# Four GNN layers in one kernel: the graph products of the second layer's next iteration are issued inside the LSTM rounds, and the third layer begins inside the last of them

## The reference, cut to what matters

```
h = relu(layernorm(x));  x = x + L0(h, adj)        # layer 1: graph product, two linear maps with batch norm
h = relu(layernorm(x));  x = x + L1(h, adj)        # layer 2: below
h = relu(layernorm(x));  x = x + L2(h, adj)        # layer 3: U = eigenvectors of the Laplacian of adj
h = relu(layernorm(x));  x = x + L3(h, adj, adj)   # layer 4: three graph products with widths 256, 512, 128

def L1(x, adj):
    h = relu(adj @ (x @ Wg0 + bg0))
    h = relu(adj @ (h @ Wg1 + bg1))
    for p in 1, 2, 3, 4:                            # windows of p neighbouring nodes
        last = LSTM_p(windows of h, p steps)        # gates i, f, g, o from Wih, Whh
        h[:, last node of each window] = last
    return h

def L2(x, adj):  U = eigh(L_norm)[1];  return U @ (relu((U.T @ x) @ W1 + b1) @ W2 + b2)
```

## Time and profile before

| | |
|---|---|
| median of 3 runs | 1040.38 us (1039.38 to 1042.43) |
| the profiled execution: its own time | 1039.46 us |
| its span, first to last instruction | 1037.7 us |
| busy: PE / PEld / DVE / ACT / POOL | 862.0 / 573.9 / 585.2 / 528.8 / 333.5 us |
| chain that ended last | PE 57%, DVE 26%, POOL 7%, ACT 6%, issue 3% |

### The profile page before, as it was taken

How to read it: one execution, slowest core, us unless ns; L and a number is a source line. 1 busy time by engine, 2 the same in 40 slices (tenths; PEclk the granted TensorE clock), 3 DMA queues, 4 the chain that set the end, 5 groups by cost and what they waited for, 6 DMA issues and landing times.

```text
span 1037.7 us, 12401 instructions
## 1 busy us (share of the span) xinstructions
PE 862.0 (83%) x3721; PEld 573.9 (55%) x3721; DVE 585.2 (56%) x3105; ACT 528.8 (51%) x962; POOL 333.5 (32%) x404
## 2 busy tenths in 40 slices
PE   2678487498879899798857858896899999999998
PEld 1444233353558546684435723575756857857856
DVE  5899867876865877488997886202503303303101
ACT  1466365375464755657526445455545545545531
POOL 1333101016555266525736316674301201201000
PEclk9999889598899999999978889998899999999999
DMA  7000000000000000000000000000000100100101
GB/s 322 0 2 1 0 0 1 1 1 1 1 1 1 1 0 2 1 1 1 0 0 1 1 1 1 1 0 1 1 1 1 41 1 1 42 0 1 42 1 40
DMA packets 2963, 13.32 MB, mean 13 GB/s; under 512 B 465, under 2 KB 465, under 8 KB 2641
## 3 DMA queue, kind: packets, MB, share of 16 engines
q1 hardware_dynamic: 2896, 12.54, 3.0%
HBM read 8.35 MB, written 4.19 MB: 12 GB/s over the span
## 4 chain that ended last, share of the span: by engine, by line
PE 57%; DVE 26%; POOL 7%; ACT 6%; issue 3%; DMA 0%; SPq 0%; DVEq 0%; ACTq 0%; POOLq 0%
PE PS L401 56%; POOL BIG L881 6%; DVE ST L1530 2%; ACT T L784 2%; DVE stats L1502 1%; ACT BIG L823 1%; DVE Fq L1322 1%; DVE seg L1323 1%; ACT T L773 1%; ACT BIG L815 1%; DVE T L1626 1%; DVE mv L1509 1%; POOL sc L861 1%; DVE sc L1063 1%; DVE vcol L1060 1%
## 5 line engine op out<-in xcount | busy, mean ns | idle before, releaser
L401 PE MATMUL PS<-BIG,wts 128*128 128x512 f32 (+2 forms) x1264 | 443.2, 507 | 41.7 <-POOL BIG L881 21.3
L401 PEld LDWEIGHTS PS<-BIG,wts 128*128 128x128 f32 x1264 | 244.4, 198 | 207.4 <-issue 123.7
L881 POOL TENSOR_TENSOR BIG<-BIG 128x256 f32<-128x256 f32 (+2 forms) x272 | 255.3, 944 | 273.2 <-ACT BIG L815 208.0
L815 ACT ACTIVATE BIG<-PS,lbias 128x256 f32<-128x256 f32 (+2 forms) x312 | 166.1, 559 | 125.7 <-PE PS L401 124.6
L1641 DVE TENSOR_TENSOR X<-X,PS 128x512 f32<-128x512 f32 x64 | 43.5, 683 | 148.7 <-PE PS L401 87.1
L722 ACT ACTIVATE BIG<-PS 128x1024 f32<-128x1024 f32 x64 | 65.5, 1024 | 88.5 <-PE PS L401 88.5
L722 ACT ACTIVATE T<-PS 128x512 f32<-128x512 f32 x96 | 55.3, 593 | 100.5 <-PE PS L401 100.3
L730 ACT ACTIVATE T<-X,shift,rstd 128x128 f32<-128x128 f32 x192 | 78.3, 481 | 43.7 <-DVE shift L1518 43.7
L401 PE MATMUL PS<-T,wts 128*128 128x512 f32 x192 | 97.3, 637 | 0.7 <-ACT T L722 0.4
L1663 DVE TENSOR_TENSOR T<-PS,wts 128x512 f32<-128x512 f32 x16 | 11.1, 692 | 150.6 <-PE PS L401 150.6
L869 POOL TENSOR_SCALAR rstd<-mv 128x4 f32<-128x4 f32 x48 | 10.9, 228 | 225.3 <-DVE mv L1509 225.3
(11 more groups left out here) (303 smaller groups left out, 1154.3 us busy)
## 6 DMA issues: line engine op xcount, KB each, us to landing
X<-x_in SPq DMA_DIRECT2D x1, 4096.0 KB, 12.6
out<-X SPq DMA_DIRECT2D x16, 256.0 KB, 2.0
wts<-w_in SPq DMA_DIRECT2D x1, 3605.5 KB, 21.7
cst<-cst_in SPq DMA_DIRECT2D x1, 419.0 KB, 3.3
AA<-adj_in SPq DMA_DIRECT2D x2, 16.0 KB, 2.0
```

What stands on the lines that cost most here:

```text
L401: return nc.tensor.matmul(o, l, r, start=start, stop=stop)
L815: nc.scalar.activation(LB[:, q, {"i": I_, "g": G_, "f": F_, "o": O_}[g], 0:n], PS[:, 3 * q + rank[q] % 3, 0:n], ACT.Tanh if g == "g" else ...
L881: nc.gpsimd.tensor_tensor(out, a, b, op).then_inc(pool_set[q], 1)
```

## The change

1. TensorE: the graph stage of iteration i+1 has no place of its own any more. Its 16 products, the four `turn` of i+1 and the four `turn_h` of i-1 are tasks that are issued within the rounds of iteration i, as the table TASKS says: half 0 of (r, q) stands behind the second gate, half 1 behind the last. All tasks write bank 7 (`task_bank`); a task waits until the engine that reads the one before it has done so (`held`). Iteration 0's graph stage stays ahead of round 0.
2. H gets a second buffer (H1, odd iterations).
3. ScalarE: the batch norm (`bn`) of the next iteration stands in round 0, the normed input in round 4, two chunks behind each set's gates, the copies and relus behind gates.
4. VectorE: the adds, biases and the next layer norm are placed for the new order. In iteration 0 the adds and stats stand ahead of the 32nd reflection, not among its instructions, and GpSimd computes the roots.
5. Layer 3's first layer norm: its stats stand in VectorE's twist, its roots on GpSimd ahead of round 7 of iteration 3 (LAST_ROOTS), its normed input on ScalarE in rounds 9 and 10. The product with BDU waits for the last tanh alone; the last four `turn_h` stand behind it, in banks of their own.
6. PACE_GRID from [40, 32] to [50, 38], PACE_TWIST from 27 to 32, PACE_SCAN from 13 to 15; SHORT_ROUND (1.6 on the clock for each set of a short round) is gone.

```
+TASKS = {
+    (0, 1, 1): ("turn", 0), (1, 0, 0): ("turn", 1), (1, 0, 1): ("turn", 2), (1, 1, 0): ("turn", 3),
...
+    (4, 1, 1): ("agg", 0), (5, 0, 0): ("agg", 1), (5, 0, 1): ("agg", 2), (5, 1, 0): ("agg", 3),
...
+NORMED = {(4, 0): (0, 1), (4, 1): (2, 3)}
+LAST_NORMED = {(9, 1): (0, 1), (10, 0): (2, 3)}
+LAST_ROOTS = 7
-PACE_GRID = [40.0, 32.0]
-PACE_TWIST = 27.0
-PACE_SCAN = 13.0
+PACE_GRID = [50.0, 38.0]
+PACE_TWIST = 32.0
+PACE_SCAN = 15.0
-SHORT_ROUND = 1.6
...
+            def task(j, name, k):
+                if held[0]:
+                    before, what, c = held[0]
+                    if what in ("agg", "agg2"):
+                        pe.wait_ge(act_done[c], C_ACT.at(before, DONE_BY[what]))
+                    else:
+                        pe.wait_ge(dve_done[c], C_DVE.at(before, DONE_BY[what]))
+                product(j, name, k, task_bank)
+                held[0] = (j, name, k)
...
+                            if at == 1 and 0 in todo:
+                                task(*todo[0])
+                        if 1 in todo:
+                            task(*todo[1])
...
                     else:
-                        for c in range(NK):
-                            pe.wait_ge(dve_done[c], C_DVE.end)
+                        for q in range(2):
+                            pe.wait_ge(act_set[q], R_ACT.start(ITER))
                     tiles(bank(k), k, T0[:, k, :], BDU[:, :])
+                if i == 0:
+                    pe.wait_ge(dve_done[NK - 1], C_DVE.end)
+                    for k in range(NK):
+                        product(ITER - 1, "turn_h", k, odd_bank(k))
...
             for i in range(ITER):
                 for r, (p, s, part) in enumerate(LSTM):
+                    if i == ITER - 1 and r == LAST_ROOTS:
+                        for k in range(NK):
+                            layer_norm_roots(0, k, D_POOL, D_DVE)
```

More of the change, by code:

```diff
@@ L146, in d_order @@
[L146 to L151, removed]
+GRAPH = ["agg", "g0", "agg2", "g1"]
+C_PE = Order(B_PE.end, [(0, n) for n in ["turn"] + GRAPH]
+             + [(j, n) for i in range(ITER) for j, names in ((i + 1, ["turn"]), (i - 1, ["turn_h"]), (i + 1, GRAPH))
+                if 0 <= j < ITER for n in names])
+C_ACT = Order(B_ACT.end, [(i, n) for i in range(ITER) for n in ["bn", "norm", "aggT", "relu0", "aggT2", "h"]])
@@ new lines, with d_order @@
+C_DVE = Order(B_DVE.end, [(0, n) for n in ["add"] + LN + ["bias0", "bias1"]]
+              + [(j, n) for i in range(ITER) for j, names in ((i + 1, ["add"]), (i - 1, ["add_h"]), (i + 1, ["bias0", "bias1"]))
+                 if 0 <= j < ITER for n in names])
+def d_order(before, front, middle, rest, ahead=(), begun=()):
+    steps = [(0, n) for n in ahead] + [(0, n) for n in begun]
+    for i in range(ITER):
+        steps += [(i, n) for n in front if (i, n) not in steps] + [(i - 1, n) for n in middle if i] + [(i, n) for n in rest]
@@ new lines, with tasks @@
+NORMED = {(4, 0): (0, 1), (4, 1): (2, 3)}
+SCALED = {(0, 0): (0, 1), (0, 1): (2, 3)}
+LAST_NORMED = {(9, 1): (0, 1), (10, 0): (2, 3)}
+LAST_ROOTS = 7
+DONE_BY = {"turn": "add", "turn_h": "add_h", "agg": "aggT", "g0": "bias0", "agg2": "aggT2", "g1": "bias1"}
+def tasks(i, r, q):
+    for part in range(2):
+        if (r, q, part) in TASKS:
+            name, k = TASKS[r, q, part]
+            j = i - 1 if name == "turn_h" else i + 1
+            if 0 <= j < ITER:
+                yield part, j, name, k
@@ L183 @@
 R_PE, R_ACT, R_POOL = lstm_steps()
+LAST_GATES = [f"{g}{len(LSTM) - 1}" for g in gates(1)[1:]]
 LEAD = 1
@@ L581, in lstm @@
                 for r, (p, s, part) in enumerate(LSTM):
+                    there[i, r, "round"] = clock[0]
                     for q in range(2):
-                        x, n = lstm_in(H, q, p, s, part)
+                        x, n = lstm_in(H(i), q, p, s, part)
+                        todo = {half: (j, name, k) for half, j, name, k in tasks(i, r, q)}
                         if r == 0:
@@ L788, in _, with bn @@
-            bn(0)
-            norm(0)
-            for i in range(ITER):
-                for k in range(NK):
-                    copy(k, T1[:, k, 0:CH], l1_bank(k), C_PE.at(i, "agg"))
-                for k in range(NK):
+            def bn(i, k):
+                act.wait_ge(pe_done[k], B_PE.end if i == 0 else C_PE.at(i - 1, "g1"))
+                nc.scalar.activation(T1[:, k, 0:CH], Y2[:, i * SG + k * CH:i * SG + (k + 1) * CH], ACT.Identity,
+                                     bias=bnv[:, 13:14], scale=bnv[:, 12:13]).then_inc(act_done[k], 1)
@@ L805, in _ @@
+            for name in GRAPH:
+                for k in range(NK):
+                    after(0, name, k, l1_bank(k))
+            for i in range(ITER):
                 rank = [0, 0]
+                late = []
                 for r, (p, s, part) in enumerate(LSTM):
-                    if r == NORM_ROUND and i + 1 < ITER:
-                        norm(i + 1)
                     for q in range(2):
-                        _, n = lstm_in(H, q, p, s, part)
+                        _, n = lstm_in(H(i), q, p, s, part)
@@ L1641, in add @@
                 v.tensor_tensor(x, x, src, ALU.add).then_inc(dve_done[k], 1)
+            for k in range(NK):
+                add(0, k, l1_bank(k), C_PE.at(0, "turn"))
+                dve.wait_ge(dve_done[k], C_DVE.at(0, "add"))
+                for _ in stats_of(0, k, C_DVE):
+                    pass
+                if k:
+                    shift_of(0, k - 1, C_POOL)
+            shift_of(0, NK - 1, C_POOL)
             l1[0] = l1_instructions()
@@ L1654, in _ @@
             for k in range(NK):
-                dve.wait_ge(dve_done[k], C_DVE.end)
-                for _ in stats_of(0, k, D_DVE, ""):
-                    pass
-            for k in range(NK):
-                shift_of(0, k, D_POOL, "")
+                add(ITER - 1, k, odd_bank(k), D_PE.at(0, "turn_h"))
             for i in range(ITER):
```

254 lines of the change are left out of this document (142 added, 112 removed), and 3 rows, old and new, of the table TASKS.

## The result

The kernel after takes 991.57 us (median of 4 runs, 991.47 to 992.19), the one before 1039.88 us on the same chip. The ratio is 0.9534, 95% interval 0.9515 to 0.9554: 48 us faster. The forecast was 996.0 us, range 980 to 1018, so it was right in sign, case and range, and 4 us too slow. Experiments ran on several chips; they are compared by their ratios to the kernel before on their own chip and by the spans of their profiled executions (before 1037.7, after 989.8).

A forecast was written before the change was run, and what follows sets the result against it. The prediction took the stage to be bound by TensorE's order, with VectorE close behind at its end. From the profiled 1039.46 us, gains of 56.4 and costs of 12.5 gave 996 us, range 980 to 1018.

The forecast's parts named there:

- Borders: Between iterations, TensorE no longer waits for the last h, the relu into H or VectorE's add: 11.7 us less.
- (d): 72 tasks share bank 7, each waiting for the reader of the one before: 4 us more.
- Short rounds and normed input: Tasks fill GpSimd waits in short rounds, 7 us less; ScalarE's normed input in two pieces, 9.3 us less.
- (b): Layer 3's normed input, 16 ScalarE activations in rounds 9 and 10 of the last iteration: 2 us more.
- Eigenvector products: Small products stand later in TensorE's order, so its waits for VectorE's chain fall from 26.1 to 15.4: 10.7 us less.
- Second: 35 against 38: none: Second grid round: VectorE needs 35 us, TensorE's products before its small product take 38, so no wait.
- Clock: Four long TensorE waits go, three at norms and one at the grid, with the slow clock behind them: 6 us less.
- Start: Iteration 0's graph stage: normed inputs are ready, agg isn't paced by ScalarE, g0 begins at about 206: 2.4 us less.
- Head: Head of layer 3: the product with BDU waits only for the last tanh, 2.0 us behind the last product: 9.3 less.
- (a): GpSimd's eight root instructions ahead of round 7 delay the next set: 4.5 us more, bounds 0 and 5.4.
- (c): Iteration 2's layer norm ends 1 to 2 us late among the grid's instructions, holding back ScalarE near round 4: 2 more.
- VectorE did not become the bound of the whole: Judges a rival (22%): from the grid on, each us VectorE is late delays the end; 1008 to 1016 us.

The follow-up runs named there:

- e3: The kernel before, with ScalarE's normed input in two pieces of eight activations behind the gates of round 7's two sets: ratio 0.9949.
- e6: The kernel after, with VectorE's add of turn_h chunk 0 in iteration 3 placed behind the request for the second grid sum: 986.37 us, ratio 0.9465.
- e9: The kernel before with the new paces (50/38, 32, 15) and iteration 2's four turn_h adds 5.0 later on the clock: 1029.68 us, ratio 0.9894.
- e4: The kernel after, with layer 3's stats, roots, normed input and the last turn_h behind the last round again: 993.07 us, ratio 0.9539.
- e5: The kernel after, with GpSimd's eight root instructions ahead of round 6 of iteration 3, not round 7: 983.86 us, ratio 0.9441.
- e10: The kernel after with GpSimd's roots ahead of round 6, the turn_h add of chunk 0 later, and PACE_TWIST 38 for 32: 976.55 us, ratio 0.9362.

## Why the prediction was right, and where not

**Borders (-11.7).** Right: what stands in their place is 2.3 us at X (counted under (d)) and 0.9 for the relu.

**Short rounds and normed input (36.2 left at 19.9).** GpSimd's two rows less the 5.4 of the roots are 19.2, so the sum is right, but by two errors that cancel. Normed input: 14.8 us became nothing, where the prediction left 4.5 (the 1.3 us at the gates stand in rounds with layer 3's normed input, so they belong to (b)). Short rounds: the three iterations with tasks went from 17.8 to 12.0, near the forecast -7, but iteration 3 rose from 3.5 to 7.1, which the prediction did not have; why it rose stays open. As reasons the two terms were right only together: e3 shows that the split alone moves most of its wait to GpSimd.

**Eigenvector products (26.1 to 15.4).** Measured 17.9. The total is near, and two terms in it are wrong. "Second: 35 against 38: none" failed: 8.2 us stand there. The step compared VectorE's work with TensorE's work and left out that VectorE may itself stand, at an add whose transpose TensorE issues later. The prediction counted the adds' 0.7 us and not their place; e6 and e9 show that this is the cause. The other way, "5.5 and 1.2" at the last EV steps became 0.9, and the sign "the wait at the last EV product is over 4" did not show. The step took 7.2 us for VectorE's last step from the trace before. It was 5.0 in the kernel after, since that price isn't the instructions' own (last section). tmp (0.8 for 0) and both_ways (8.0 for 7) were right.

**Clock (-6).** Too small. With the same 3721 matmul instructions, PE's busy time fell from 862.0 to 852.1:

```profile
PE 852.1 (86%) x3721; PEld 565.9 (57%) x3721; DVE 583.2 (59%) x3095; ACT 522.6 (53%) x962; POOL 339.6 (34%) x412
```

That is 9.9 us, which I put down to the clock: iterations 1 and 2 are granted 1.00 and 0.98 where the earlier trace rows has 0.97 and 0.89. The prediction counted four waits that go. What the rest comes from, for one the many short waits that went, no run separates.

**Start (-2.4).** Wrong: nothing came of it. Round 0 begins 0.25 us later than before; first the kernel before, then after:

```profile
221.33 5.39 PE L401 MATMUL PS<-BIG,wts 128*128 128x512 f32 x12 [0.95 <-ACT BIG L800]
```

```profile
202.20:208.60 6.40, 6.40 (x34) 6.40 (x34) 5.49 (x38) 1.79 (x3) 0.00 (x0) 0.55 0.00 0
221.58 2.81 PE L431 MATMUL PS<-BIG,wts 128*128 128x512 f32 x6 [0.95 <-ACT BIG L842]
```

The step that failed is "`agg` isn't paced by ScalarE". ScalarE is indeed out of the way there (busy 1.79 us of 6.40; 6.00 of 6.10 before), and `agg` still takes 6.55 us for 6.19, at a granted clock of 0.55 (0.59 before), behind a wait of 10.47 us for the 32nd reflection. So `g0` begins at 208.58 and not at 206.

**Head (-9.3).** 9.8 by e4 against the kernel after (11.4 became 1.84), so right.

**What it adds (+12.5).** (a) The roots cost 5.4 for 4.5, and some 2.5 of clock; e5 shows that another round makes them free. (b) 1.3 for 2. (c) ScalarE waited 1.4 us for the late layer norm in iteration 2; what it cost wasn't isolated. (d) 2.3 us at X and 0.4 at ScalarE's copies for 4; that "a copy or an add fits in" held for nearly all of the 72 tasks.

**The rivals.** VectorE did not become the bound of the whole: from 202 to 662 us it waits 36.5 us for TensorE in the reflections (50.2 before) and 11.7 at X. The warning sign of the prediction, a VectorE over 95% busy from the grid on while TensorE waits, did not show: from xg's wait to both_ways (564.8 to 616.9) it is busy for 47.7 of 52.1 us, or 91%. At xg it had been idle before. At both_ways it is the limit, as the prediction said: on the way there it waits only 1.8 us for TensorE. One bank was enough. Iterations 0 to 2 were said to take 112 us and took 107; the last product was put near 669 and ended at 667.52. So the sum was right partly by luck: three iterations were some 14 us better and the last, 124 us to its last product, some 10 us worse than the forecast implies. By terms, the clock and the normed input came out some 8 us better, and the eigenvector products, the start and the waits for GpSimd some 10 us worse; the smaller terms were not measured one by one.

## What to carry to other kernels

When two in-order engines take turns, read both views of a wait: an engine that is waited for may itself be holding the place of something that the first issues later, and then moving one add past one request may be all it takes (here 7 us of 991). Moving work ahead to shorten a head is paid where it lands; put it in a wait that exists anyway (here 9 us of span lay between two neighbouring rounds). Don't add the gains of parts measured alone: the paces gave 2 us in one order and 19 in the other.

## What the runs showed of the hardware

The length of a small VectorE instruction depends on GpSimd beside it, by far more than the earlier trace rows had shown. The same two instructions of the last eigenvector step, in the kernel before:

```profile
650.02 1.21 DVE L1432 TENSOR_TENSOR EV<-EV 64x64 f32<-64x64 f32 x1
651.26 1.30 DVE L1433 TENSOR_TENSOR EV<-EV 64x64 f32<-64x64 f32 x1
```

in the kernel after:

```profile
659.35 0.71 DVE L1499 TENSOR_TENSOR EV<-EV 64x64 f32<-64x64 f32 x1
660.10 0.68 DVE L1500 TENSOR_TENSOR EV<-EV 64x64 f32<-64x64 f32 x1
```

and in e10:

```profile
650.51 0.22 DVE L1500 TENSOR_TENSOR EV<-EV 64x64 f32<-64x64 f32 x1
...
```

GpSimd's instructions beside them are of 512 columns in the kernel before (1.30 us each), of 256 in the kernel after (0.73 each), and in e10 there are none. So in these rows a VectorE instruction of 0.22 us that meets a GpSimd one takes about as long as that one: 1.21 or 1.30, 0.71 or 0.68, and 0.22. The step's length follows, 7.3, 5.0 and 3.8 us. It works the other way too: beside VectorE's wide instructions GpSimd's multiplication takes 2.26 to 2.52 us for 1.29 (e6). The Trainium skill ("SBUF — State Buffer", "Who interferes with whom") has a GpSimd instruction and a VectorE one with two SBUF inputs, or in a two-port mode, exclude each other for the whole length of an instruction. The TENSOR_TENSOR rows agree, with the lengths given; in which mode the TENSOR_SCALAR and the COPY of e10 ran, no trace shows.
